# Level 64's products beside the next step's first small ones, the solve behind the first projection, and a hint on the closing branch, in a gated delta-rule kernel

## The reference, cut to what matters

```python
qkvz = hidden_states @ W_qkvz                     # 256 columns in
y = silu(conv_depthwise(mixed, conv_w))           # 4 taps along the tokens; gives q, k, v
q = repeat(l2norm(q), 2) * DK ** -0.5 ; k = repeat(l2norm(k), 2)
def step(S, inp):
    qt, kt, vt, gt, bt = inp
    S = S * exp(gt)
    delta = (vt - einsum('hk,hkv->hv', kt, S)) * bt
    S = S + kt[:, :, None] * delta[:, None, :]
    return S, einsum('hk,hkv->hv', qt, S)
gated = core * silu(z)
gated = gated * rsqrt(mean(gated * gated) + EPS) * norm_w
return gated @ W_out
```

## Time and profile before

| | us |
|---|---|
| median of 3 runs | 3241.34 |
| the profiled execution, its own time | 3238.56 |
| its span, first to last instruction | 3236.9 |
| TensorE busy (MATMUL) | 3052.3 (94%) |
| VectorE busy | 2370.4 (73%) |
| ScalarE busy | 1787.5 (55%) |
| GpSimd busy | 1690.2 (52%) |

### The profile page before, as it was taken

How to read it: one execution, slowest core, us unless ns; L and a number is a source line. 1 busy time by engine, 2 the same in 40 slices (tenths; PEclk the granted TensorE clock), 3 DMA queues, 4 the chain that set the end, 5 groups by cost and what they waited for, 6 DMA issues and landing times. The chain is left out here.

```text
span 3236.9 us, 70170 instructions
## 1 busy us (share of the span) xinstructions
PE 3052.3 (94%) x23017; PEld 2230.3 (69%) x23017; DVE 2370.4 (73%) x4933; ACT 1787.5 (55%) x5786; POOL 1690.2 (52%) x3745
## 2 busy tenths in 40 slices
PE   5997699999999999999999999999999999978998
PEld 4555477777777777777777777767777777764555
DVE  3443578888878877887888788878887888745776
ACT  4222466666656665665666566656665666532332
POOL 1000566666666666666666666666666666620000
PEclk9999899999999999999999999999999999988999
DMA  3000111211111111111111112212111111110000
GB/s 75 1 1 20 27 42 37 47 43 39 43 39 43 36 43 36 42 36 43 36 42 36 43 36 45 46 35 46 42 39 40 39 43 35 36 48 1 7 7 14
DMA packets 447077, 113.98 MB, mean 35 GB/s; under 512 B 350496, under 2 KB 445840, under 8 KB 446672
## 3 DMA queue, kind: packets, MB, share of 16 engines
q1 hardware_dynamic: 446672, 108.98, 15.0%
HBM read 63.85 MB, written 45.09 MB: 34 GB/s over the span
## 5 line engine op out<-in xcount | busy, mean ns | idle before, releaser
L1135 DVE SCALAR_TENSOR_TENSOR conv<-raw,ckq,conv 128x512 f32<-128x512 f32 x384 | 343.7, 908 | 18.8 <-ACT conv L878 9.6
L1135 DVE SCALAR_TENSOR_TENSOR conv<-raw,cv,conv 128x512 f32<-128x512 f32 x384 | 297.2, 788 | 9.1
L877 ACT ACTIVATE raw<-bank 128x512 f32<-128x512 f32 x256 | 153.0, 598 | 271.7 <-PE bank L671 271.5
L467 POOL TENSOR_TENSOR Tb<-Tb,btmp 64x14 f32<-64x14 f32 (+6 forms) x896 | 258.5, 288 | 70.8 <-POOL btmp L463 1.2
L463 POOL TENSOR_TENSOR btmp<-Bk,Tb 64x14 f32<-64x14 f32 (+6 forms) x896 | 254.8, 284 | 65.7
L525 PE MATMUL bank<-S,ykq 128*128 128x256 f32 x1024 | 252.5, 391 | 28.7 <-issue 28.7
L671 PE MATMUL bank<-xnT,wkq 128*128 128x512 f32 x512 | 259.4, 631 | 12.8 <-DMA ckq<-in_L_attn_conv_w_dram 10.3
L1081 DVE SCALAR_TENSOR_TENSOR N<-ET,ty,bank 128x128 f32<-128x128 f32 x512 | 143.7, 343 | 163.4 <-POOL ET L409 163.3
L671 PE MATMUL bank<-xnT,wv 128*128 128x512 f32 x512 | 255.1, 621 | 4.3 <-issue 4.3
L740 PE MATMUL bank<-wout_h,gT 128*128 128x256 f32 x1024 | 245.6, 383 | 3.0 <-ACT gT L897 3.0
L688 PE MATMUL bank<-wz_h,xnT 128*128 128x256 f32 x1024 | 242.4, 380 | 0.0
(11 more groups left out here) (350 smaller groups left out, 7903.9 us busy)
## 6 DMA issues: line engine op xcount, KB each, us to landing
blk_n<-N SPq DMA_DIRECT2D x128, 256.0 KB, 2.8
Tp<-blk_t SPq DMA_DIRECT2D x128, 128.0 KB, 2.9
Wp<-blk_w SPq DMA_DIRECT2D x128, 128.0 KB, 2.9
wkq<-in_L_attn_W_qkvz_dram SPq DMA_DIRECT2D x32, 128.0 KB, 2.2
wv<-in_L_attn_W_qkvz_dram SPq DMA_DIRECT2D x16, 256.0 KB
Bk<-blk_n SPq DMA_DIRECT2D x64, 64.0 KB, 2.7
blk_t<-Tb SPq DMA_DIRECT2D x64, 64.0 KB, 2.5
blk_w<-Wb SPq DMA_DIRECT2D x64, 64.0 KB, 2.5
```

What stands on the lines that cost most here:

```text
L467: pool.tensor_tensor(Tb[:, j + 1:, 0:j], Tb[:, j + 1:, 0:j], tmp, ALU.subtract).then_inc(row_rdy, 1)
L877: act.activation(raw[h][:, j, :, 3:], bB[1 - j], ACT.Copy)
L1135: dve.scalar_tensor_tensor(out=conv[h][:, j], in0=raw[h][:, j, :, k:k + 256], scalar=cw[:, j, k:k + 1], in1=conv[h][:, j], op0=ALU.mult, o ...
```

## The change

It has four parts, all in `delta_rule`.

1. `pipeline` asks for a hint on the closing branch of each engine's loop. It puts one instruction (BRANCH_PREFETCH_HINT) at the top of each turn of the loop on every engine.
2. `x64` is done one slot later (lag 6 in place of 5) and stands ahead of `x16`; `w64` stands behind `w1`. Both write to halves of PSUM banks (`bG[4]`, `bG[5]`) that are free there. `xev64` on ScalarE and `add_w64` on VectorE are moved accordingly: `xev64` now stands between `from_state` and `norms`.
3. `solve` stands behind `project(s, 0)`, and `w2` and `values` stand between `solve` and `apply`.
4. ScalarE's `evac`, `vscale`, `kdec`, `squares` and VectorE's `uscale`, `add_w2`, `add_w3` change places to suit: `uscale` now stands behind `strict`, `add_w2` ahead of `update`, `add_w3` between the two halves of the taps.

```diff
-            with eng.Fori(1, STEPS // SLOTS) as i:
+            with nc.Fori(1, STEPS // SLOTS, engines=[eng.engine], hint_back_edge=True) as i:
...
 def x16(s):
-                    wait(pe, xs64_rdy, before)
 def w1(s):
-                    wait(pe, w64_rdy, before)
+                    wait(pe, xs64_rdy, before)
 def x64(s):
-                    t = s.back(S_L)
+                    t = s.back(S_L + 1)
+                    wait(pe, w3_rdy, done)
-                        i = pe.matmul(bH[5][64:, u], N[t.c % RING][0:64, u, 64:], T[0:64, u, :], start=True, stop=True)
+                        i = pe.matmul(bG[4][64:, u], N[t.c % RING][0:64, u, 64:], T[0:64, u, :], start=True, stop=True)
 def w64(s):
-                    wait(pe, w3_rdy, done)
-                        i = pe.matmul(bH[4][0:64, u], Xs64[64:, u, :], Wf[64:, u, 64:], start=True, stop=True)
+                        i = pe.matmul(bG[5][0:64, u], Xs64[64:, u, :], Wf[64:, u, 64:], start=True, stop=True)
...
                 def body(s):            # TensorE
                     state_in(s)
-                    w64(s)
+                    x64(s)
                     x16(s)
                     front(s)
+                    w1(s)
+                    w64(s)
+                    project(s, 0)
                     solve(s)
-                    w1(s)
+                    w2(s)
+                    values(s)
                     apply(s)
-                    values(s)
-                    w2(s)
-                    project(s, 0)
+                    project(s, 1)
                     w3(s)
-                    project(s, 1)
-                    x64(s)
                     gated_tp(s)
...
                     from_state(s)       # ScalarE
+                    xev64(s)
                     norms(s)
                     expo(s)
                     normed(s)
+                    evac(s, 0)
+                    vscale(s)
                     kdec(s)
-                    vscale(s)
-                    evac(s, 0)
+                    evac(s, 1)
                     squares(s)
-                    evac(s, 1)
-                    xev64(s)
                     gtev(s)
...
                     rhs(s)              # VectorE
-                    add_w64(s)
                     gate(s)
                     xev16(s)
                     silu(s)
-                    uscale(s)
+                    add_w64(s)
                     add_w1(s)
                     strict(s)
+                    uscale(s)
+                    add_w2(s)
                     update(s)
-                    add_w2(s)
                     output(s)
-                    add_w3(s)
                     attention(s)
                     taps(s, 0)
+                    add_w3(s)
                     taps(s, 1)
```

More of the change, by code:

```diff
@@ L536, in x16 @@
                     T, Nt = Tp[t.c // 2 % 2][:, t.c % 2], N[t.c % RING]
-                    loaded, before = held(pe, t.pairs(32, 32)), held(pe, t.done(1))
+                    loaded = held(pe, t.pairs(32, 32))
                     pe.wait_ge(m["made"], 2)
                     wait(pe, t_in, loaded)
-                    wait(pe, xs64_rdy, before)
                     for u in range(U):
@@ L886, in xev64 @@
                     act.wait_ge(x64_mm, t.done())
-                    act.activation(Xs64[64:], bH[5][64:], ACT.Copy, scale=-1.0).then_inc(xs64_rdy, 1)
+                    act.activation(Xs64[64:], bG[4][64:], ACT.Copy, scale=-1.0).then_inc(xs64_rdy, 1)
                 def gtev(s):
@@ L951, in add_w64 @@
                     dve.wait_ge(w64_mm, t.done())
-                    dve.tensor_copy(Wf[0:64, :, 64:], bH[4][0:64]).then_inc(w64_rdy, 1)
+                    dve.tensor_copy(Wf[0:64, :, 64:], bG[5][0:64]).then_inc(w64_rdy, 1)
                 def accumulate(s):
```

## The result

| | before | after |
|---|---|---|
| median, us (4 runs each) | 3242.24 | 3290.43 |
| lowest to highest | 3238.70 to 3244.12 | 3288.43 to 3293.85 |
| profiled execution's span | 3236.9 | 3286.7 |
| first product of the first slot, L525 | 390.64 | 396.67 |
| from there to the last slot's | 2481.9 | 2525.6 |

A forecast was written before the change was run, and what follows sets the result against it. TensorE set the 19.26 us slot, with the taps loop close behind at 18.07; the change makes that loop the bound. 3238.56 + 101 (slots) - 37 (hint) = 3302.6, plus 2.8 for the median: 3305, range 3262 to 3368.

The forecast's parts named there:

- the loop over the taps: VectorE's last tap, SiLU, sums, `derive`, `strict`, `uscale`, `update`, taps: from 18.07 to 20.04 us mean, setting the slot.
- The first leg: From a slot's last VectorE tap to `strict`: 7.19 us before, +0.30 for `xev64` moved ahead of `norms`.
- `strict` to E: From `strict` to E, the end of a slot's last VectorE tap: net +1.67 us from `uscale` and `add_w2` moving.
- the rival of cancelling: Taps overlap GpSimd less and shrink, slot grows 0.3 us, hint gives all back: about 3237; chance 4%.
- The slot: +0.84 forecast: Mean delta-rule slot, 19.26 us before, taken as 20.1; 120 slots make +101 us.
- GpSimd: `squares` to next `strict`: at most 0.3 us more in half the slots; as rival 3353, chance 6%.
- C': Not forecast; follow-ups' two-slot loop: `derive`, block inverse, memory trip, `x16`, `expo`, `strict`, taps, SiLU, sums; 41.40 us.
- TensorE's list: TensorE's work per slot: pairing small groups saves about 0.30 us, leaving about 18.8 of 20.1 us.
- The waits at L670: TensorE waits for `ET` at L670 and `Us` at L710 in nearly every slot, together over 1 us.
- The hint: Closing branches: six edges lose 41 us; the hint gives back 37, with 0 and 41 as ends.
- the rival by which the hint does nothing: Closing branches: about 108 ns per branch makes six edges worth 0.65 us; time 3342; chance 12%.
- TensorE stays the bound: Rival: the grouping pays, slots 18.79 us, -56 and -41 for the hint: 3144; chance 8%.

The follow-up runs named there:

- the first repair: Kernel after, with `uscale` moved ahead of `strict` on VectorE: 3372.89 us, ratio 1.0391.
- the placed runs: Kernel before and changed order, both without the hint, every engine's loop starting at a code block's start: 3208.51 us and 3288.21 us.
- the tuned pairs: Kernel after keeping its pairs; `solve`, `apply` ahead of first projection, `uscale` ahead of `strict`, `add_w3` ahead of taps, `squares` ahead of first `evac`: 3203.66 us.
- the new order, placed: Kernel after without the hint, with every engine's loop starting at the start of a code block: 3288.21 us, ratio 1.0137.

## Why the prediction was right, and which terms were off

The mechanism was the one forecast: the loop over the taps sets the slot, and TensorE gets slack. The median came out 15 us below the forecast: the slots were priced 29 us too high, and some 14 us came at places that were put at less.

*What bounds the kernel.* That VectorE's idle time is latency inside a loop 1.2 us shorter than TensorE's slot was the right reading. With the loop 1.8 us longer (19.86 for 18.07) the slot grew by 0.60 us and TensorE got slack.

*The first leg: +0.30 for `xev64` was too small.* It measured 0.57 (3.00 - 2.43). I took the operation's 0.38 less an overlap, and there is none: `xev64` starts when `from_state` is over (1659.63), where the sums used to begin 0.15 us sooner, and the sums start 0.41 us behind it. Taking it out again gave 41 us. The whole leg: 7.67 and 7.78 for 7.49.

*`strict` to E: right in one slot by luck, 0.93 too long in the other.* With q/k's taps 12.01 us against 20.43 - 7.49 = 12.94. The six q/k taps took 5.58 us before because GpSimd's `gtri` stood beside one of them, and I kept that number. Moving `update` moved the taps against `gtri`: now it runs at 1693.27 beside `add_w3`'s small operations, takes 1.04 instead of 1.54 us, and the taps take 2.56 + 2.33, which is 0.69 less. With v's taps 12.16 against 19.64 - 7.49 = 12.15, but there the taps grew, 2.32 + 2.72 for 4.79, since GpSimd's L451 now holds one of them up: 0.25 more. In both slots two small terms of the sum were too long: from the end of `strict` to `update` it is 1.93 us in place of 2.00, and where VectorE no longer waits ahead of `add_w3` its neighbours overlap again, 0.18 us that the waits of 0.79 and 0.83 don't contain. In the v slot these 0.25 us less and the taps' 0.25 more cancel. In the mean of the two slots 0.46 us are missing, 0.22 of them in the taps. The prediction names the taps under the rival of cancelling, as a slot that grows by 0.3 us only. Behind a loop top `gtri` meets a tap again (3.30 us for three taps, at 1570.77), which is part of why those slots are long.

*The slot: +0.84 forecast, +0.60 measured.* The taps loop was put at 20.04 us, to which I added 0.06 for GpSimd. It measured 20.04 + 0.24 (the leg, 7.73 in the mean for 7.49) - 0.46 (`strict` to E) = 19.81 in the pair shown, 19.86 as the median. 120 slots by 0.60 make 72 us where 101 stood. The q/k and v slots were to differ by up to 0.8 us; they differ by 0.16 in the median.

*GpSimd.* It doesn't set the slot in the kernel after, but had 0.42 us left, and it is what the first repair ran into, by the other loop C'. Its term, at most 0.3 us in half the slots, came to nothing. What the estimate did not contain is that the loop's length depends on who stands beside it.

*TensorE's list.* 19.03 busy in place of 18.8. The pairs are worth at most 0.17 us a slot where 0.30 was taken from the lengths of single groups. The waits at L670 (0.36, in every second slot) and L710 (0.30 and 0.65) came where they were expected, and inside the loop, not on top, but they are 0.66 us a slot together where over 1 us was said. The clock in the pair of slots shown stayed at 1.00.

*The hint.* -37 was forecast, out of 41 for six edges like the first one; the six cost 44.8 us, and in the kernel after 10.0, which is -35. That this came out is luck for the most part. The new order without the hint has edges of 16.1 us in all: 28.7 of the 34.8 come with the new order's code, by its position as the placed runs suggest, and 6.1 with the hint, which against the order alone shortened the run by 4 us. On the kernel before it brought 45. So the two terms are not parts of a sum. The forecast's +64 against the profiled execution came out as +50: -29 for the slots, +2 for the edges, +6 ahead of the first slot, which I had at nothing, and +6 in single longer slots, two behind the loop's entry, a few inside the loop and the last ones. The Trainium skill gives a compare-and-branch about 108 ns ("Advanced Engine Details and Errata", Control Flow Timing), and from it came the rival by which the hint does nothing. The runs differ: on the kernel before the same branch cost 6.6 to 8.2 us without the hint and 0.1 to 0.9 with it.

*The rivals.* That TensorE stays the bound (3144) fell: L525 is 19.86 us apart, and even in the tuned pairs, where `uscale` and `solve` are back in their places, the shortest slots are 19.09 and not 18.79.

## What to carry to other kernels

An engine with a quarter of its time idle can still be a microsecond from being the bound: follow one of its waits back round the engines until it closes on itself, and put every moved operation into that loop or outside it before pricing it. Where two engines run large operations side by side, durations are not properties of the operation but of the neighbour, so price a moved step with the neighbours it gets. Try the cheap half of a change by itself, the loop's hint here: bundled, its 45 us disappeared under an order that cost 91. And compare two versions of a loop with its code placed alike, or a shift of the code is read as an effect of the edit.

## What the hardware showed that was not expected

- The gap behind a taken closing branch depends on where the loop's code begins: 4.76 us and 1.75 us in front of the same product, from the same instructions in the loop. That placement is worth 36 us here, and the hint 45, with what it shifts.
- After a gap the granted clock may or may not fall, and the length of the gap doesn't decide it: over 4 us it is 1.00 behind 1.75 and 1.94 us, 0.61 behind 2.07 us (`uscale` first) and 0.68 behind 2.06 us (the new order, placed), 0.57 behind 4.76 us. In the placed new order all six branches have a gap of about 2 us; behind two of them (917.5 and 1877.6 us) the clock is 0.68 and 0.57, behind the other four 1.00.

```profile
917.50:921.50 4.00, 3.87 (x32) 3.01 (x32) 2.23 (x6) 2.51 (x7) 1.99 (x8) 0.68 0.03 8
```

  That is the window behind the first of these six.
- VectorE and GpSimd stretch each other: a GpSimd 128x512 `gtri` 1.04 or 1.54 us, its 64x256 scaling 1.07 or 1.62, its 64x26 row sum 0.23 or 0.71, the longer when it starts while a 128x512 tap runs; three taps 2.32 or 3.30. Which side pays is a matter of hundredths: the scaling of 1.07 us in the kernel after starts 0.01 us ahead of a tap, and then it is the tap that takes 1.15 us in place of 0.75; the scaling of 1.62 us starts 0.07 us behind a tap.
- A wait for DMA of 2 us once in two slots cost more than itself where the clock fell behind it: `x16` took 1.12 us in place of 0.68.
